# A graph attention kernel: in one of its two max-subtracting steps, the row maxima reach all partitions through DRAM instead of through TensorE

## The reference, cut to what matters

```
def layer(h, params):
    wl, b_l, ws, b_s, wr, b_r, g, beta = params
    u = jnp.einsum('bid,bjd->bij', h, h) / temper
    a = jax.nn.softmax(u, axis=-1)
    delta = a * adjacency_matrix
    attn = delta / (jnp.sum(delta, axis=-1, keepdims=True) + 1e-10)
    hl = h @ wl.T + b_l
    hs = h @ ws.T + b_s
    hr = h @ wr.T + b_r
    diag_a = jnp.diagonal(attn, axis1=1, axis2=2)
    ctx = (jnp.einsum('bij,bjd->bid', attn * upper, hl) + diag_a[..., None] * hs
           + jnp.einsum('bij,bjd->bid', attn * lower, hr))
    ...
    o = (ctx - mean) / jnp.sqrt(var + LN_EPS) * g + beta
    return (jax.nn.relu(o), None)
...
x = x + _L0_gnn_ref(h, adj, ...)        # h = relu(layernorm(x))
```

## Time and profile before

| | |
|---|---|
| runs | 1179.71, 1180.22, 1180.55 us; median 1180.22 us |
| profiled execution | 1179.74 us, span 1178.0 us |
| TensorE (PE) | 1167.0 us busy, 99% of the span, 6998 matmuls |
| VectorE (DVE) | 939.7 us busy, 80% |
| GpSimd (POOL) | 639.4 us busy, 54% |
| ScalarE (ACT) | 495.0 us busy, 42% |
| granted TensorE clock | 0.999 of full speed |
| DMA | 80.55 MB, 20.1% of the 16 engines' span on SP's queue |

### The profile page before, as it was taken

The page is one execution under the profiler, slowest core; times in us unless marked ns, Lnnn a source line. Parts: engine busy times, 40 slices in busy tenths (PEclk is TensorE's granted clock), DMA queues, the critical chain, the costliest instruction groups (busy, mean ns, idle before and its releaser), DMA issues.

```text
span 1178.0 us, 18565 instructions
## 1 busy us (share of the span) xinstructions
PE 1167.0 (99%) x6998; PEld 1158.1 (98%) x6998; DVE 939.7 (80%) x1872; ACT 495.0 (42%) x1065; POOL 639.4 (54%) x669
## 2 busy tenths in 40 slices
PE   9999999999999999999999999999999999999997
PEld 7999999999999999999999999999999999999997
DVE  6778986689866988769887598876988769875688
ACT  5346433364343543444334443344333454335532
POOL 4685463654635556445555456554475544754347
PEclk9999999999999999999999999999999999999999
DMA  7521312013121131211212112211212113110000
GB/s 245 187 66 55 116 55 81 22 52 117 55 81 37 36 117 55 81 37 62 91 55 81 37 68 85 67 68 37 88 66 81 55 36 113 41 54 1 1 28 27
DMA packets 43481, 80.55 MB, mean 68 GB/s; under 512 B 6912, under 2 KB 24832, under 8 KB 43392
## 3 DMA queue, kind: packets, MB, share of 16 engines
q1 hardware_dynamic: 43104, 78.98, 20.1%
q10 hardware_dynamic: 288, 0.39, 0.1%
HBM read 66.72 MB, written 12.64 MB: 67 GB/s over the span
## 4 chain that ended last, share of the span: by engine, by line
PE 97%; DVE 2%; issue 0%; DMA 0%; ACT 0%; POOL 0%; DVEq 0%
PE rot_ps L344 17%; PE rot_ps L343 17%; PE rot_ps L342 17%; PE u_ps L342 14%; PE u_ps L344 14%; PE u_ps L343 14%; PE rot_ps L405 2%; PE u_ps L398 2%; PE rot_ps L414 1%; DVE xt_sb L670 0%; DMA x_norm<-x_dram 0%; DVE hs L774 0%; DVE z L754 0%; DVE stats L780 0%; DVE x_stats L615 0%
## 5 line engine op out<-in xcount | busy, mean ns | idle before, releaser
L950 POOL TENSOR_TENSOR hw_lo<-proj,hw_hi 128x384 fp32r<-128x384 f32 x256 | 281.6, 1120 | 280.3 <-ACT hw_hi L530 280.3
L342 PE MATMUL rot_ps<-w_hi,ht_hi 128*128 128x384 f32 x1152 | 389.2, 338 | 0.0
L344 PE MATMUL rot_ps<-w_hi,ht_lo 128*128 128x384 f32 x1152 | 385.4, 335 | 0.0
L343 PE MATMUL rot_ps<-w_lo,ht_hi 128*128 128x384 f32 x1152 | 385.2, 334 | 0.0
L343 PEld LDWEIGHTS rot_ps<-w_lo,ht_hi 128*128 128x128 f32 x1152 | 216.5, 188 | 0.0
L342 PEld LDWEIGHTS rot_ps<-w_hi,ht_hi 128*128 128x128 f32 x1152 | 216.5, 188 | 0.0
L344 PEld LDWEIGHTS rot_ps<-w_hi,ht_lo 128*128 128x128 f32 x1152 | 216.2, 188 | 0.0
L505 ACT ACTIVATE u_off<-u_ps 128x128 f32<-128x128 f32 (+1 forms) x128 | 42.5, 332 | 393.7 <-PE u_ps L344 393.5
L717 DVE TENSOR_TENSOR proj<-rot_ps,bias 128x384 f32<-128x384 f32 x256 | 140.1, 550 | 47.4 <-PE rot_ps L344 45.7
L962 POOL TENSOR_TENSOR dg<-et_hi,tri 128x256 fp32r<-128x256 f32 x128 | 113.5, 887 | 94.5 <-PE u_ps L344 94.5
L530 ACT ACTIVATE hw_hi<-proj 128x384 fp32r<-128x384 f32 x256 | 127.9, 520 | 66.0 <-DVE proj L717 66.0
(11 more groups left out here) (89 smaller groups left out, 2038.7 us busy)
## 6 DMA issues: line engine op xcount, KB each, us to landing
out_dram<-z SPq DMA_DIRECT2D x64, 192.0 KB, 1.9
x_norm<-x_dram SPq DMA_DIRECT2D x15, 768.0 KB, 4.3
xt_sb<-x_t_dram SPq DMA_DIRECT2D x15, 768.0 KB, 4.5
adj_a<-adj_t_dram SPq DMA_DIRECT2D x8, 1024.0 KB, 5.4
adj_b<-adj_t_dram SPq DMA_DIRECT2D x8, 1024.0 KB, 5.4
x_norm<-rows_dram SPq DMA_DIRECT2D x15, 512.0 KB, 3.8
x_a<-x_dram SPq DMA_DIRECT2D x8, 768.0 KB, 4.6
x_b<-x_dram SPq DMA_DIRECT2D x8, 768.0 KB, 4.6
```

Source lines behind the costliest of these rows:

```text
L342: pe.matmul(dst, a_hi, b_hi, start=first and m == 0, stop=False)
L343: pe.matmul(dst[:, 0:b_lo.shape[1]], a_hi, b_lo, start=False, stop=False)
L344: done = pe.matmul(dst, a_lo, b_hi, start=False, stop=last and m == n - 1)
L950: pool.tensor_tensor(hw_lo[:, t, n, :], proj[:, t % 2, n, :], hw_hi[:, t, n, 0:dim].bitcast(F32), ALU.subtract).then_inc(hw_lo_done, 1)
```

## The change

In step 2 alone, the unit M and ScalarE's copy go. In their place:

- `neg_max` becomes 32 columns wide (four of them hold the maxima) and lives, with a second such tile `max_turned`, in `diag_junk`, a scratch tile that exists already;
- after the four `row_max`, VectorE transposes the 128x32 in blocks of 32x32. Now partition 32q+t, for q and t from 0 to 3, holds the maxima of rows 32q to 32q+31 of tile t;
- SP stores these rows with four DMAs of 4 rows of 128 bytes each into `max_dram` (DRAM, 512 values), waits until all four have landed, and reads `max_dram` back into `m_rows`, to all 128 partitions;
- `shift_scores(0)` waits for this read (`max_spread`) instead of for ScalarE's copy.

Step 3 keeps M. The rotation of the banks has one unit less in a pair.

```
-    ORDERS = [UNITS_0, UNITS_0 + TURN, UNITS_1 + TURN, UNITS_1]
+    ORDERS = [UNITS_0, UNITS_0 + TURN, UNITS_0 + TURN, UNITS_1]
...
-    N_M = (0, 0, 1, 1)
+    N_M = (0, 0, 0, 1)
...
+    TURN32 = 32
...
-        neg_max = sb("neg_max", [P, TILES])
...
+        neg_max = diag_junk[:, 3, 0:TURN32]
+        max_turned = diag_junk[:, 3, TURN32:2 * TURN32]
...
+        max_dram = nc.dram_tensor("max_dram", [1, n_rows], F32, kind="Internal").ap()
...
                 if not last:
                     sp.wait_ge(xt_scaled, KB * next_a)
                     spread_x_rows(next_b)
+                sp.wait_ge(max_turned_done, it + 1)
+                by_quarter = max_dram[0].rearrange("(t g r) -> g t r", t=TILES, r=TURN32)
+                for quarter in range(P // TURN32):
+                    sp.dma_start(by_quarter[quarter],
+                                 max_turned[quarter * TURN32:quarter * TURN32 + TILES, :]).then_inc(max_stored, 16)
+                sp.wait_ge(max_stored, 64 * (it + 1))
+                sp.dma_start(m_rows, max_dram[0:1, :].to_broadcast([P, n_rows])).then_inc(max_spread, 16)
...
                     round_proj(0)
-                    copy_max()
+                    if s == 3:
+                        copy_max()
                     exp(0)
...
                 def shift_scores(t):
-                    if t == 0:
+                    if t == 0 and s == 2:
+                        dve.wait_ge(max_spread, 16 * (it + 1))
+                    elif t == 0:
                         dve.wait_ge(m_copied, at(it, s, 1, N_M))
...
                     for t in range(TILES):
                         row_max(t)
+                    if s == 2:
+                        dve.wait_ge(max_done, at(it, s, TILES, N_E))
+                        dve.transpose(max_turned[:, :], neg_max[:, :]).then_inc(max_turned_done, 1)
                     evacuate(0, 1)
```

More of the change, by code:

```diff
@@ L157, in build_digcn @@
         row_sum_done = sem("row_sum_done")
+        max_turned_done = sem("max_turned_done")
+        max_stored = sem("max_stored")
+        max_spread = sem("max_spread")
         m_ready = sem("m_ready")
```

## The result

| | before | changed |
|---|---|---|
| median | 1180.06 us (4 runs) | 1201.65 us (4 runs, 1199.44 to 1202.60) |
| profiled execution, span | 1179.74, 1178.0 us | 1201.66, 1199.9 us |
| PE busy, matmuls | 1167.0 us, 6998 | 1170.4 us, 6966 |
| mean granted clock | 0.999 | 0.995 |

The ratio is 1.0178, 95% interval 1.0166 to 1.0191: slower, by 21.6 us. The forecast was 1204 us, in a range from 1195 to 1221.

What follows compares the result with a forecast made beforehand. PE was taken to bound the kernel (97% of the span), with zero slack in VectorE's work behind the shift. Transpose, stores and read delay the shift 3.0 us per pair, 24 us in eight: 1204 us, range 1195 to 1221.

Steps and rivals of the forecast that it cites:

- Zero slack: Step 2, VectorE's work behind the shift: no idle time, so a shift x later makes PE x later.
- M's removal worth nothing in the changed kernel: Step 2, PE: without M (0.35 to 0.44 us per pair) PE only arrives earlier at the T it must wait for.
- Four issues: SP's stores into max_dram: the fourth is issued 1.35 us after the first (bounds 1.15 and 1.6).
- Landing of the stores: After the last store's issue: 1.8 us until the stores have landed in DRAM (bounds 1.5 and 3.0).
- The read: 256 KB from max_dram into 128 partitions: 2.7 us (bounds 1.9 and 3.8).
- Where PE stands: Step 2: 0.4 us before P(1,2), some tenths at the next two, about 2.2 us before the second T.
- The sum: The shift starts at 100.9 instead of 97.88: 3.0 us later per pair, 24 us in eight pairs.
- rival B: Round trip longer (5.4 us, 1223 us in all) or TensorE's clock falls (13 us more, 1217 us); chance 0.24.
- main case: A: the round trip makes the shift 2.2 to 3.9 us later, 1197 to 1211 us; chance 0.62.
- Rival D: The round trip is hidden, fitting into 2.5 us; PE gains 0.44 us per pair, 1176 us; chance 0.03.
- Rival E: PE has unseen slack before T, so part or all of the loss vanishes: 1176 to 1182 us; chance 0.03.
- Rival C: Cheaper but still slower: shift 1.6 us later, 1192.5 us, or e_low returns 1.2 us, 1194 us; chance 0.08.

Runs made afterwards that it cites:

- e5: The changed kernel with the read from DRAM done twice, the second after the first has landed: 1224.01 us, ratio 1.0371.
- e7: The changed kernel with evacuate(1,2) moved ahead of e_low(2) and evacuate(2,2) ahead of e_low(3) in the third step: 1192.03 us, ratio 1.0102.
- e1: The changed kernel without transpose and stores; one DMA fills m_rows early from a row of the adjacency, not the maxima: 1175.87 us, ratio 0.9962.
- e6: The kernel before with evacuate(1,2) moved ahead of e_low(2) and evacuate(2,2) ahead of e_low(3) in the third step: 1179.89 us, ratio 0.9996.
- e3: The changed kernel with one store of all 128 partitions in place of four of 4 rows: 1197.43 us, ratio 1.0147.
- e9: The kernel of e8 with the first two triangles ahead of GpSimd's last low parts in the third step: 1179.96 us, ratio 0.9998.
- e10: The kernel before, M kept and no round trip, with all order changes of e9 on VectorE, ScalarE and GpSimd: 1184.71 us, ratio 1.0037.
- e8: The changed kernel with one store, e7's order, evacuate(2,0) and (2,1) ahead of the shift, projection rounding ahead of ScalarE's exponentials: 1177.96 us, ratio 0.9982.

## Why the prediction was right, step by step

- **Zero slack** behind the shift, read from a stretch that was 13.01 us busy of 13.01: right, within 0.03 us in five pairs, and at 5.45 us in the mean of e5. e7 shows the other side: the place that held PE was the one named, the T units behind `e_low`.
- **M's removal worth nothing in the changed kernel**: right. PE arrives early and waits. e1 gives its worth where nothing is late, 4.1 us, a little more than the 3.5 us in the sum for D; the 0.07 us a pair of e6 are the difference.
- **Transpose**: 0.25 us expected with its wait; it ended at 95.13, 0.24 us behind the last maximum. **SP's reaction**: first store 0.03 us later, as expected.
- **Four issues**: 1.35 us expected from first to fourth. They are issued 0.33 us apart (1.29 us for all four): 1.0 us, below my lower bound of 1.15. The row I took the pace from had larger transfers.
- **Landing of the stores**: 1.8 us expected, lower bound 1.5. The last landed 1.17 us after its issue. Together with the issues these are the mis-sized terms: 1.0 us too much.
- **The read**: 2.7 us expected, 3.0 to 3.3 measured. Half the bytes of the larger spread took only a tenth less than its shortest, 3.4 us; taking 0.9 us off for the bytes was wrong, and by these two sizes most of the time doesn't depend on them. The Trainium skill's page "DMA: Bandwidth & Descriptors", section "Anatomy of one DMA — SWDGE (gpsimd) path", gives 2.6 us by the estimate that I set beside mine, and is as far off.
- **Where PE stands**: right for the main stop, before the second T, 1.97 us where 2.2 were expected. The small ones were expected before `P(1, 2)` and the next two; there is one, before `P(3, 2)`. The shift came earlier than in the sum, and evacuate(2,1) with it: in the first pair it ended at about 104.4, before `P(1, 2)` wanted its bank.
- **The sum**: shift late by 3.0 us expected, 2.34 us in the mean: 24 us expected, 18.7 measured. The clock, which I had as half of rival B at 13 us, added 3.1 us. So 1204 against 1201.65 us is close in part by luck: stores too dear, read too cheap, and no clock in the sum offset each other. One sign that was named as speaking against the prediction did show: behind the stop the matmuls of pairs 1 and 4 are 0.32 us apart and not 0.175. It is these 3.1 us that the sum of the main case lacked.
- **Rival D** (hidden) decided at 3.0 us behind the transpose; the numbers came 5.4 us behind it. **Rival E** is refuted by the table. **Rival C**, with e_low giving something back: from the shift to the last evacuations VectorE took 11.51 us after 11.53 before, so nothing came back. **Rival B**'s long trip did not come; its clock did, at a quarter of the price. It ran low for 3.4 us each time, at a loss of 1.5 us, near what I had assumed for one fall; but it fell in two pairs and not in eight.

What stays open: why the clock fell in pairs 1 and 4 and not in the six others, with stops between 1.94 and 1.98 us in all of them. Nor is the stop alone enough: all four executions of the changed kernel have a lower mean clock than before, of e3's four only one has.

## What to carry to other kernels

Work is free to leave the engine that bounds the kernel only if its result still comes in time. Before such an exchange, follow the consumer's stream from the waiting instruction to the next thing that the bounding engine takes from it, and add up its idle time there; if there is none, the whole added latency is lost in every iteration. If the detour is wanted all the same, put work that doesn't need its result ahead of the wait, and let go of the buffers first: here that turned 21.6 us of loss into about 2 us of gain. And before a reordering is judged by its time, look at each iteration: in e9 and e10 one operation on VectorE, side by side with one on GpSimd, took 0.68 us in some pairs and 1.55 in others, and hid what the reordering gave.

## What the runs showed of the hardware

- Four stores of 512 bytes went out 0.33 us apart, and the last had landed 1.17 us after its issue; behind one store of 16 KB the read that waited for it was issued after 1.95 us. A broadcast read of 256 KB from DRAM into SBUF took 3.0 to 3.3 us, one of 512 KB 3.4 at least.
- In the profiled executions a stop of 1.94 to 1.98 us before transposes was followed by half the clock, for 3.4 us, in two of eight cases in the changed kernel and in none of eight in e3; in e5 a stop of 2.0 to 2.3 us before projections was followed by it in eight of eight.
- One operation of VectorE, `e_low` with two SBUF inputs, took 0.68 us beside an idle GpSimd (105.71 in e8). Begun together with GpSimd's `hw_lo` it took either 0.68 us, with 1.56 for `hw_lo`, or 1.5, with 1.0 for `hw_lo`. By the page "SBUF — State Buffer" of the Trainium skill, section "SBUF: two separate sides", the two engines share a port pair as an exclusive lock, and whichever of two such operations starts first has it for the whole instruction. The durations agree with that, since one of the two goes at full pace and the other takes 0.5 to 0.9 us more, though no run here tested the port by itself.
